# Experts over 512 tokens with a transposed sum, and small work of the attention moved off VectorE

## The chip, the cores and the metric

The kernel runs on one core of a Trainium2 chip. The metric is the time of the core for one execution, in microseconds (us). The engines are PE (TensorE, with PEld for its weight loads), DVE (VectorE), ACT (ScalarE), POOL (GpSimd) and SP (SyncE, which here only issues transfers). Each runs its own list of instructions in order and waits for the others on semaphores.

## The reference

One transformer layer on x of shape (2, 1024, 128): causal attention with 16 heads of 8 dimensions, where the heads of q and k are normalised and rotated, and then a mixture of 16 experts, of which a router picks 2 for each token, beside a shared expert.

```python
x = x + attn(_layernorm(x))
x = x + ffn(_layernorm(x))
# attn: q, k, v = x @ W.T by heads; q, k = layernorm(q), layernorm(k), then rope
scores = where(causal, scale * q @ k.T, -inf); attn = softmax(scores); out = attn @ v @ Wo.T + bo
# ffn: all experts are computed, combine holds the router's two weights of a token
h = silu(xf @ We1 + be1) * (xf @ We3 + be3)
yo = einsum('tei,eid->ted', h, We2) + be2
y = einsum('te,ted->td', combine, yo)
z = silu(xf @ ws1 + bs1) * (xf @ ws3 + bs3) @ ws2 + bs2
```

## The kernel before

The 2048 tokens are four chunks x = 0 to 3 of 512 (two to a sequence). Each chunk passes these stages. Preparation: layernorm, q, k and v, the deviations of the heads (`head_rstd`: an inverse root by three Newton steps on 128 values per partition), rope, and the split of q and k into three bf16 parts that transfers stack up in `q_st` and `k_st`. Attention, in four groups of four heads per chunk, so 16 groups a = 0 to 15: "max" units compute scores with queries on the partitions (L753, L759) and DVE reduces them to row maxima (L1157). DVE negates and splits these (`max_negate`), PE turns them (L770), DVE copies them (`max_copy`, L1176) and a transfer puts them into `q_st` as extra rows, so that the second computation of the scores (L783) comes out with the maximum subtracted. ACT takes the exponential of two banks at once (L911), POOL masks the diagonal, and PE multiplies with v (L801, "pv"). Epilogue: output projection, second layernorm, router (`route1` to `route3`, some 40 small DVE instructions in a chain), and the weights of the experts, which go to memory and come back spread over the partitions (`cstore`, `cload`). Experts: the 16 are 8 pairs, with the shared one 9 units.

Before the change a chunk has 18 expert steps: 9 units for each half of 256 tokens. In each, PE computes the two products U and V into the two halves of one PSUM bank (L838, L839), ACT copies both out with their biases (L948, L950) and takes the tanh (L958), DVE forms (1 + tanh) * U (L1246), V is multiplied with the token's expert weight (L601, on POOL for chunks 0 to 2 and on DVE for chunk 3), POOL multiplies the two (L1076), and PE adds the result into the sum bank with the h tile as stationary operand (L850, two tiles of 128 tokens), so tokens come out on the partitions. The rings of h, U and V hold 4 tiles. The shared expert's two steps come first; the other 16 need the weights from `cload`, which is issued in halves.

The order on each engine is made by a planner in the file, `plan()`: it takes dependences, lengths of each step and an urgency from tables of windows (`PREP_WINDOWS`, `MAX_WINDOWS`, `MOE_WINDOWS`, `PV_LAG`) and writes one list, `SCHEDULE`, from which each engine takes its own steps in order. PSUM has 8 banks: 7 collects pv, 6 the experts' sum, and banks 0 to 5 go to pairs for scores and maxima; single fills (projections, transposes, experts) take 5, 4, 3 or 2. A bank is free again when its reader has read it (`FILLS_READ`).

## Time and profile before

| | |
|---|---|
| three runs | 459.22, 461.11, 461.4 us; median 461.11 |
| the profiled execution | 462.71 us, its span 461.0 us |
| granted TensorE clock, mean | 0.89 of 2.4 GHz |
| busy | PE 387.2, DVE 352.2, ACT 273.4, POOL 186.8 us |
| instructions recorded | 7965 |

The span is the time from the first to the last recorded instruction; 1.7 us of the execution lie outside it. Busy times are of one execution. A matmul's end is modelled in the records, so a PE that shows as full isn't at its peak.

The chain of work that ended last is 55% PE and 25% DVE. The attention's last transposes end near 397 us; what follows is the experts of chunks 2 and 3.

### The profile page before, as it was taken

The numbers are of one execution on the slowest core, as the hardware profiler recorded it, in microseconds if no ns is written. First come the engines' busy times: TensorE is split into PE (matmuls) and PEld (weight loads), VectorE is DVE, ScalarE is ACT, GpSimd is POOL, SyncE is SP. The second block draws the span as 40 slices with busy tenths as digits, with TensorE's granted clock in tenths as the row PEclk, the third lists the DMA queues.
The fourth block names the chain that finished last, engine by engine and source line by source line (L and its number), as shares of the span: only waits on it lengthen the run. The fifth ranks groups of instructions, "written<-read, shape, count | busy, mean of one in ns | idle before, by whom it ended". The sixth has DMA issues, their size and how long they took to land.

```text
span 461.0 us, 7965 instructions
## 1 busy us (share of the span) xinstructions
PE 387.2 (84%) x2663; PEld 194.1 (42%) x2663; DVE 352.2 (76%) x757; ACT 273.4 (59%) x483; POOL 186.8 (41%) x277
## 2 busy tenths in 40 slices
PE   3642867679797999999999798889999999986995
PEld 2321322213323443664334334544333273775884
DVE  4778989889878788794387799987875883678396
ACT  2523044621786584757955664439688789864784
POOL 1303926732065225464523130546202244575564
PEclk9765698575889699999999699999999999999998
DMA  5955022000050007000005005300000000800530
GB/s 144 193 101 137 2 60 79 3 1 0 1 138 1 3 19 169 1 1 1 4 23 139 2 1 126 63 1 1 2 2 0 1 3 4 197 11 1 143 67 23
DMA packets 30265, 21.54 MB, mean 47 GB/s; under 512 B 8945, under 2 KB 30098, under 8 KB 30162
## 3 DMA queue, kind: packets, MB, share of 16 engines
q1 hardware_dynamic: 28834, 19.99, 18.6%
q10 hardware_dynamic: 1392, 1.05, 0.9%
q8 instruction: 22, 0.36, 0.4%
q14 instruction: 17, 0.14, 0.1%
HBM read 13.43 MB, written 1.18 MB: 32 GB/s over the span
## 4 chain that ended last, share of the span: by engine, by line
PE 55%; DVE 25%; ACT 8%; issue 7%; POOL 2%; SPq 1%; DMA 1%; POOLq 0%; ACTq 0%; DVEq 0%
PE psum L801 13%; PE psum L783 7%; PE psum L759 7%; PE psum L850 6%; DVE mx_diag L1157 6%; PE psum L838 6%; PE psum L839 5%; DVE mx_full L1157 3%; PE psum L753 3%; PE psum L724 3%; ACT probs L911 2%; DVE nr L1095 2%; DVE mv L601 2%; DVE nr L1096 2%; PE psum L733 1%
## 5 line engine op out<-in xcount | busy, mean ns | idle before, releaser
L911 ACT ACTIVATE probs<-psum 128x1024 f32<-128x1024 f32 x144 | 141.6, 1027 | 58.7 <-PE psum L783 55.4
L1157 DVE TENSOR_REDUCE mx_diag<-psum 128x4 f32<-128x512 f32 (+2 forms) x96 | 96.6, 1039 | 26.4 <-PE psum L759 25.8
L1065 POOL TENSOR_SCALAR_AFFINE_SELECT probs<-probs 128x256 f32<-128x256 f32 (+1 forms) x112 | 47.7, 442 | 108.3 <-ACT probs L911 107.8
L1157 DVE TENSOR_REDUCE mx_full<-psum 128x2 f32<-128x1024 f32 x64 | 75.8, 1218 | 17.0 <-PE psum L759 16.7
L1076 POOL TENSOR_TENSOR mh<-mh,mv 128x256 f32<-128x256 f32 x72 | 55.5, 777 | 77.9 <-DVE mh L1246 69.5
L801 PE MATMUL psum<-probs,v_ones 128*9 128x512 f32 (+3 forms) x768 | 82.1, 519 | 1.5 <-POOL probs L1065 0.8
L783 PE MATMUL psum<-q_st,k_st 64*128 64x512 bf16 (+3 forms) x384 | 59.8, 363 | 9.7 <-ACT probs L911 6.7
L759 PE MATMUL psum<-k_st,q_st 62*128 62x512 bf16 (+3 forms) x384 | 62.7, 357 | 4.4 <-DVE mx_full L1157 2.3
L1246 DVE SCALAR_TENSOR_TENSOR mh<-mh,mu 128x256 f32<-128x256 f32 x72 | 36.5, 523 | 27.0 <-ACT mh L958 26.7
L948 ACT ACTIVATE mu<-psum,b1h 128x256 f32<-128x256 f32 x72 | 33.8, 470 | 37.0 <-PE psum L839 25.0
L850 PE MATMUL psum<-w,mh 128*128 128x128 f32 x288 | 48.1, 295 | 5.6 <-POOL mh L1076 5.5
L838 PE MATMUL psum<-x2T,w 128*128 128x256 f32 x144 | 47.7, 414 | 1.6 <-ACT mv L950 1.6
L601 POOL TENSOR_TENSOR mv<-mv,comb_b 128x256 f32<-128x256 f32 x48 | 35.4, 740 | 27.7 <-ACT mv L950 23.9
L850 PEld LDWEIGHTS psum<-w,mh 128*128 128x128 f32 x288 | 39.3, 194 | 17.3 <-POOL mh L1076 9.5
L839 PE MATMUL psum<-x2T,w 128*128 128x256 f32 x144 | 43.8, 387 | 0.0
L783 PEld LDWEIGHTS psum<-q_st,k_st 64*128 64x128 bf16 x384 | 17.5, 97 | 59.9 <-ACT probs L911 38.8
L753 PE MATMUL psum<-causal_bf,ident_bf 128*128 128x128 bf16 (+1 forms) x192 | 33.1, 259 | 10.3 <-DVE mx_diag L1157 7.1
L950 ACT ACTIVATE mv<-psum,b 128x256 f32<-128x256 f32 x72 | 33.8, 469 | 0.0
L958 ACT ACTIVATE mh<-mu 128x256 f32<-128x256 f32 x72 | 29.7, 418 | 6.8 <-PE psum L855 2.8
L759 PEld LDWEIGHTS psum<-k_st,q_st 62*128 62x128 bf16 x384 | 16.4, 95 | 35.1 <-issue 16.1
L839 PEld LDWEIGHTS psum<-x2T,w 128*128 128x128 f32 x144 | 28.2, 196 | 4.2
L753 PEld LDWEIGHTS psum<-causal_bf,ident_bf 128*128 128x128 bf16 x192 | 13.4, 101 | 39.1 <-DVE mx_diag L1157 18.6
(142 smaller groups left out, 422.4 us busy)
## 6 DMA issues: line engine op xcount, KB each, us to landing
comb_b<-combine_scratch SPq DMA_DIRECT2D x16, 512.0 KB, 8.7
q_st<-parts SPq DMA_DIRECT2D x24, 128.0 KB, 2.5
k_st<-parts SPq DMA_DIRECT2D x18, 128.0 KB, 2.4
w<-in_We SPq DMA_DIRECT2D x3, 512.0 KB
k_st<-in_c_pad SPq DMA_DIRECT2D x2, 512.0 KB, 8.0
out<-xs SPq DMA_DIRECT2D x4, 256.0 KB, 4.5
xs<-in_x SPq DMA_DIRECT2D x3, 256.0 KB, 10.3
k_st<-parts ACTq DMA_DIRECT2D x6, 128.0 KB, 3.5
```

The source lines that it names most:

```text
L601: engine.tensor_tensor(mv[:, at % MOE_RING, :], mv[:, at % MOE_RING, :], comb_b[:, half, u, :], ALU.mult).then_inc(weighted, 1)
L753: pe.matmul(v, ident_bf[:, :], causal_bf[:, :].unsqueeze(1).broadcast_to([P, nm, P]), start=True, stop=False, skip_group_check=True)
L759: last = pe.matmul(w[:, par, i * keys:(i + 1) * keys], q_st[r, x % 2, 2 * g + m, q0:q0 + P], k_st[r, b, 2 * g + m, k0:k0 + keys], start=(w ...
L783: last = pe.matmul(w[:, par, col:col + cols], k_st[rows(par), b, 2 * g + m, kt * P:(kt + 1) * P], q_st[rows(par), x % 2, 2 * g + m, q0:q0 ...
L801: last = pe.matmul(acc[32 * j:32 * j + VC, q0:q0 + cols], v_ones[:, b, kt, G * g + j, :], probs[:, n % P_RING, j % 2, col:col + cols], sta ...
L838: pe.matmul(w[:, 0:HALF], w1[:, u, :], rhs, start=True, stop=True)
L839: pe.matmul(w[:, HALF:CH], w3[:, u, :], rhs, start=True, stop=True).then_inc(work_full, 1)
L850: last = pe.matmul(y[:, tok * P:(tok + 1) * P], mh[:, at % MOE_RING, t * P:(t + 1) * P], w2[:, u, :], start=(n == 0 and t == 0), stop=(n = ...
L911: act.activation(probs[:, n % P_RING, :, :], wpair("scores", (s, i)), ACT.Exp, scale=SCALE).then_inc(exp_done, 1)
L1065: last = pool.affine_select(out=v, in_=v, compare_op=ALU.is_ge, fill=0.0, base=0, pattern=[[0, v.shape[1]], [1, P]], channel_multiplier=-1)
L1076: pool.tensor_tensor(mh[:, at % MOE_RING, :], mh[:, at % MOE_RING, :], mv[:, at % MOE_RING, :], ALU.mult).then_inc(h_ready, 1)
L1157: dve.tensor_reduce(dst[:, qt, :, pairs[0]:pairs[0] + nm], w, AX.X, ALU.max).then_inc(max_free, 1)
```

## The change

The experts run over all 512 tokens of a chunk at once, 9 units instead of 18 steps. U and V have a bank each (`moeV`, `moeU`). ACT reads V with its bias, halved (`moe_v`); the tanh is read from U's bank, and a second ACT instruction adds 1 (`moe_t`). DVE reads U from PSUM again, adds the bias and multiplies with V (`moe_a`, and this frees U's bank). POOL multiplies with 1 + tanh (`moe_g`), and then POOL, in chunk 3 DVE, multiplies with the expert weight (`moe_h`). The ring of h holds 9 tiles, so a chunk can have all its products ready before its weights arrive. The sum is transposed: the weights w2 are the stationary operand and h the moving one (`moe_sum`), so the sum bank has the output's dimension on the partitions; ACT copies it out (`y_leave`), PE turns it back (`yturn`), DVE adds it. `cload` is two transfers of the whole chunk, not four of halves.

For chunks 1 to 3 the deviations of the heads go from DVE to POOL, in 15 instructions, and rope on POOL is in two steps, so that other steps can stand between. The row maxima are negated by the reduction itself; the split goes to POOL (`max_split`), the copy of the turned maxima to ACT (`mcopy`), and the buffer of the maxima is doubled, so that the next group's reduction waits for the split two groups back. The seed of each inverse root takes one instruction instead of two. All windows of the planner are new.

```diff
-P_RING, MOE_RING = 6, 4
+P_RING, V_RING, T_RING = 6, 4, 9
...
-PV_LAG = 49.3
...
+PV_LAG = 152.8
+WEIGHT_OF = ("moe_h", "moe_h", "moe_h", "moe_h_dve")
+ROPE_OF = (("headrstd", "rope"),) + (("rstd_pool", "rope_pool", "rope_join"),) * 3
...
         def weight(engine, x, n):
 
-            at, (half, u) = 2 * UNITS * x + n, unit(n)
-            if u == 0:
-                engine.wait_ge(ld_combine[half], 32 * (x + 1))
-            engine.wait_ge(act_u, at + 1)
-            engine.tensor_tensor(mv[:, at % MOE_RING, :], mv[:, at % MOE_RING, :], comb_b[:, half, u, :],
-                                 ALU.mult).then_inc(weighted, 1)
+            u = unit(n)
+            if n == 1:
+                engine.wait_ge(ld_combine, 32 * (x + 1))
+            engine.wait_ge(gate_done, UNITS * x + n + 1)
+            h = mh[:, (UNITS * x + n) % T_RING, :]
+            engine.tensor_tensor(h, h, comb_b[:, u, :], ALU.mult).then_inc(weighted, 1)
...
-                rhs = x2T[:, x % 2, half * HALF:(half + 1) * HALF]
-                pe.matmul(w[:, 0:HALF], w1[:, u, :], rhs, start=True, stop=True)
-                pe.matmul(w[:, HALF:CH], w3[:, u, :], rhs, start=True, stop=True).then_inc(work_full, 1)
+                pe.matmul(w, (w1 if kind == "moeU" else w3)[:, unit(n), :], x2T[:, x % 2, :], start=True, stop=True
+                          ).then_inc(work_full, 1)
...
-                pe.wait_ge(h_ready, at + 1)
-                for t in range(2):
-                    tok = 2 * half + t
-                    last = pe.matmul(y[:, tok * P:(tok + 1) * P], mh[:, at % MOE_RING, t * P:(t + 1) * P], w2[:, u, :],
-                                     start=(n == 0 and t == 0), stop=(n == 2 * UNITS - 1), skip_group_check=True)
+                    pe.wait_ge(gate_done, at + 1)
+                else:
+                    pe.wait_ge(weighted, PAIRS * x + n)
+                last = pe.matmul(y, w2[:, unit(n), :], mh[:, at % T_RING, :], start=(n == 0), stop=(n == UNITS - 1),
+                                 skip_group_check=True)
                 if n == BIAS_STEP:
                     pe.wait_ge(work_read_act, frees("act", turned("cT", x)))
-                    for t in range(TPC):
-                        last = pe.matmul(y[:, t * P:(t + 1) * P], combT[:, t * P:(t + 1) * P], b2[:, :],
-                                         start=False, stop=False, skip_group_check=True)
+                    last = pe.matmul(y, b2[:, :], combT[:, :], start=False, stop=False, skip_group_check=True)
                 last.then_inc(y_done, 1)
...
-                if at >= MOE_RING:
-                    act.wait_ge(h_ready, at - MOE_RING + 1)
-                act.activation(mu[:, at % MOE_RING, :], wbank("moe", (x, n))[:, 0:HALF], ACT.Identity,
-                               bias=b1h[:, u:u + 1], scale=0.5)
-                act.activation(mv[:, at % MOE_RING, :], wbank("moe", (x, n))[:, HALF:CH], ACT.Identity,
-                               bias=b3[:, u:u + 1]).then_inc(act_u, 1)
+                if at >= V_RING:
+                    act.wait_ge(gate_done, at - V_RING + 1)
+                act.activation(mv[:, at % V_RING, :], wbank("moeV", (x, n)), ACT.Identity,
+                               bias=b3h[:, unit(n):unit(n) + 1], scale=0.5).then_inc(work_read_act, 1)
...
+                at = UNITS * x + n
+                act.wait_ge(work_full, turned("moeU", (x, n)))
+                if at >= T_RING:
+                    act.wait_ge(y_done, at - T_RING + 1)
+                t = mh[:, at % T_RING, :]
+                act.activation(t, wbank("moeU", (x, n)), ACT.Tanh, bias=b1h[:, unit(n):unit(n) + 1], scale=0.5
+                               ).then_inc(act_t, 1)
+                act.wait_ge(act_t, 2 * at + 1)
+                act.activation(t, t, ACT.Identity, bias=ones_col[:, 0:1]).then_inc(act_t, 1)
...
+                    act.copy(maxT[:, arg % 2, :], wbank("mturn", arg).bitcast(BF16)[0:8, 0:CH]).then_inc(work_read_act, 1)
...
+                elif kind == "y_leave":
+                    act.wait_ge(y_done, UNITS * (arg + 1))
+                    if arg >= 1:
+                        act.wait_ge(work_full, turned("yturn", arg - 1))
+                    act.copy(yT[:, :], bank(Y_BANK)).then_inc(y_left, 1)
...
+            def head_rstd(x):
+                pool.wait_ge(sums_ready, x)
+                y = seed_pool[:, :].bitcast(F32)
+                v, t, h = [nr_pool[:, i, :] for i in range(3)]
+                link(pool.tensor_scalar(v, ssum[:, :], 1.0 / HD, EPS, ALU.mult, ALU.add))
+                link(pool.tensor_scalar(seed_pool[:, :], v.bitcast(I32), -0.5, RSQRT_SEED, ALU.mult, ALU.add))
+                link(pool.tensor_scalar(v, v, -0.5, None, ALU.mult))
+                for step in range(3):
+                    link(pool.tensor_tensor(t, y, y, ALU.mult))
+                    link(pool.tensor_tensor(h, t, v, ALU.mult))
+                    link(pool.tensor_scalar(t, h, 1.5, None, ALU.add))
+                    link(pool.tensor_tensor(y if step < 2 else hrstd[:, :], y, t, ALU.mult))
+
...
+            def max_split(a):
+                c = a // NG % 2
+                if c:
+                    pool.wait_ge(min_ready, NG * (a // NG // 2) + a % NG + 1)
+                else:
+                    pool.wait_ge(max_free, MAXES[a, len(max_units_of(c)) - 1] + 1)
+                m = mx_diag[:, a % 2, :, :, :]
+                if a >= 1:
+                    pool.wait_ge(work_full, turned("mturn", a - 1))
+                hi, lo = [negmax[:, :, :, r, :] for r in range(2)]
+                link(pool.tensor_copy(hi, m))
...
+                    pool.wait_ge(u_read, at + 1)
+                    t = mh[:, at % T_RING, :]
+                    pool.tensor_tensor(t, t, mv[:, at % V_RING, :], ALU.mult).then_inc(gate_done, 1)
...
-                link(dve.tensor_scalar(seed[:, 0:n], v.bitcast(I32), 1, None, ALU.logical_shift_right))
-                link(dve.tensor_scalar(seed[:, 0:n], seed[:, 0:n], -1, RSQRT_SEED, ALU.mult, ALU.add))
+                link(dve.tensor_scalar(seed[:, 0:n], v.bitcast(I32), -0.5, RSQRT_SEED, ALU.mult, ALU.add))
...
+                if u == 0 and a >= 2:
+                    dve.wait_ge(neg_ready, a - 1)
...
-                link(dve.tensor_scalar(hi, m, -1.0, None, ALU.mult))
-                dve.scalar_tensor_tensor(out=lo, in0=m, scalar=-1.0, in1=hi,
-                                         op0=ALU.mult, op1=ALU.subtract).then_inc(neg_ready, 1)
...
+                dve.tensor_reduce(dst[:, a % 2, qt, :, pairs[0]:pairs[0] + nm], w, AX.X, ALU.max, negate=True).then_inc(max_free, 1)
...
+                dve.wait_ge(act_t, 2 * at + 2)
+                v = mv[:, at % V_RING, :]
+                dve.scalar_tensor_tensor(out=v, in0=wbank("moeU", (x, n)), scalar=b1[:, unit(n):unit(n) + 1], in1=v,
+                                         op0=ALU.add, op1=ALU.mult).then_inc(u_read, 1)
...
+                    dve.wait_ge(work_full, turned("yturn", arg))
+                    dve.tensor_tensor(xs[:, arg, :, :], wbank("yturn", arg).rearrange("p (t d) -> p t d", t=TPC),
+                                      xs[:, arg, :, :], ALU.add).then_inc(work_read_dve, 1)
```

The order on DVE before, from the sum of squares of chunk 1 (ssum) to the first groups' maxima (mx_diag); nr, seed and hrstd belong to the deviations of the heads, negmax and maxT to the maxima:

```order
L1128 TENSOR_REDUCE ssum<-sq 128x128
L1132 TENSOR_SCALAR hvar<-ssum 128x128
...
L1097 SCALAR_TENSOR_TENSOR hrstd<-nr,seed 128x128
L1157 TENSOR_REDUCE mx_diag<-psum 128x4 x2
L1157 TENSOR_REDUCE mx_diag<-psum 128x2 x4
L1168 TENSOR_SCALAR negmax<-mx_diag 128x8x2
L1169 SCALAR_TENSOR_TENSOR negmax<-mx_diag,negmax 128x8x2
L1157 TENSOR_REDUCE mx_diag<-psum 128x4 x2
L1176 COPY maxT<-psum 8x512
```

The same place on DVE now:

```order
L1168 TENSOR_REDUCE ssum<-sq 128x128
L1292 MEMSET ones_col 128x1
L1293 TENSOR_SCALAR b3h<-b 128x9
L1294 TENSOR_SCALAR b1h<-b 128x9
L1199 TENSOR_REDUCE mx_diag<-psum 128x4 x2
L1199 TENSOR_REDUCE mx_diag<-psum 128x2 x4
L1199 TENSOR_REDUCE mx_diag<-psum 128x4 x2
L1199 TENSOR_REDUCE mx_diag<-psum 128x2 x4
L1199 TENSOR_REDUCE mx_diag<-psum 128x4 x2
L1199 TENSOR_REDUCE mx_diag<-psum 128x2
L1184 TENSOR_TENSOR resid<-psum,parts 128x512
```

The twelve instructions of the deviations, the two of the split and the copy are gone, and fifteen reductions now stand in a row before the remainder of chunk 1's q (resid).

The order on POOL now at that place, from the last parts of chunk 0 to those of chunk 1 (before, L582 to L593 followed L1047 directly):

```order
L1076 TENSOR_TENSOR parts<-resid,parts 128x512 x2
L1051 TENSOR_SCALAR nr_pool<-ssum 128x128
...
L1058 TENSOR_TENSOR hrstd<-seed_pool,nr_pool 128x128
L587 TENSOR_TENSOR qk<-qk,hrstd 128x1024
L590 TENSOR_TENSOR sq<-qk,g_cos 128x1024
L593 TENSOR_TENSOR roped<-qk,g_sin 128x16x32 x2
L1070 CAST negmax<-mx_diag 128x8x2
L1071 TENSOR_TENSOR negmax<-mx_diag,negmax 128x8x2
L600 TENSOR_TENSOR sq<-sq,g_add 128x1024
L601 TENSOR_TENSOR roped<-roped,sq 128x1024
```

The deviations stand ahead of rope, and the split of group 0's maxima stands between rope's two steps.

The end of PE's order now, from the transpose of chunk 3's expert weights (lg) on; L844 is U or V of a unit, L855 the sum, L859 the biases of the experts, L732 the turn of the sum:

```order
L835 MATMUL psum<-ident,lg 16x128 x4
L855 MATMUL psum<-mh,w 128x512
L844 MATMUL psum<-x2T,w 128x512 x9
L855 MATMUL psum<-mh,w 128x512
L844 MATMUL psum<-x2T,w 128x512 x2
L855 MATMUL psum<-mh,w 128x512
L732 MATMUL psum<-ident,yT 128x128 x4
L855 MATMUL psum<-mh,w 128x512
L859 MATMUL psum<-combT,b 128x512
L855 MATMUL psum<-mh,w 128x512 x7
L732 MATMUL psum<-ident,yT 128x128 x4
```

Before, U and V of chunk 3's steps (L838, L839) alternated with sums (L850) to the end; now all U and V stand ahead of the last eight sums.

## Rows read from the trace of the kernel before

**Rows 1.** Stretches: busy us of PE, PEld, DVE, ACT, POOL; clock, DMA share, GB/s

```profile
40.00:110.00 70.00, 51.48 (x316) 18.10 (x316) 63.33 (x109) 23.46 (x40) 34.70 (x35) 0.70 0.13 32
110.00:160.00 50.00, 44.19 (x304) 17.73 (x302) 39.88 (x90) 31.06 (x49) 20.32 (x25) 0.79 0.12 33
160.00:398.00 238.00, 222.88 (x1706) 104.41 (x1705) 177.66 (x350) 164.78 (x258) 85.41 (x148) 0.97 0.13 32
398.00:461.00 63.00, 52.86 (x304) 45.08 (x302) 44.12 (x110) 40.81 (x104) 38.10 (x50) 0.95 0.26 62
```

**Rows 2.** PE's longest waits, 40 to 110 us and 160 to 250 us: total, times, longest

```profile
PE psum L753 <- DVE mx_diag L1157: 6.5, 10, 2.4
...
PE psum L783 <- ACT probs L911: 1.3, 2, 0.9
```

**Rows 3.** DVE in order of time, 42 to 78 us: start, us, instruction

```profile
42.09 0.23 DVE L1132 TENSOR_SCALAR hvar<-ssum 128x128 f32<-128x128 f32 x1
...
46.43 0.29 DVE L1097 SCALAR_TENSOR_TENSOR hrstd<-nr,seed 128x128 f32<-128x128 f32 x1
...
52.48 0.78 DVE L1168 TENSOR_SCALAR negmax<-mx_diag 128x16 bf16<-128x16 f32 x1
...
55.24 0.40 DVE L1176 COPY maxT<-psum 8x512 bf16<-8x512 bf16 x1
...
76.78 1.29 DVE L1168 TENSOR_SCALAR negmax<-mx_diag 128x16 bf16<-128x16 f32 x1
```

**Rows 4.** POOL in order of time, 21 to 47 us

```profile
21.61 0.45 POOL L566 TENSOR_TENSOR g_add<-g_add,g_tmp 128x128 f32<-128x128 f32 x1
...
46.80 2.34 POOL L582 TENSOR_TENSOR qk<-qk,hrstd 128x1024 f32<-128x1024 f32 x1 [2.85 <-DVE hrstd L1097]
```

**Rows 5.** PE of L838, then L839, then L850 alone, in 160 to 398 us

```profile
160.00:398.00 238.00, 27.27 (x80) 12.85 (x80) 0.97 0.13 32
...
160.00:398.00 238.00, 23.73 (x78) 15.35 (x79) 0.97 0.13 32
...
160.00:398.00 238.00, 26.16 (x152) 20.06 (x152) 0.97 0.13 32
```

**Rows 6.** The chain of waits in order of time: start, us, what; 188 to 189 us

```profile
188.33 0.63 PE psum L838 x2
188.96 0.43 PE psum L839 x2
```

**Rows 7.** The chain of waits, 425 to 461 us

```profile
425.60 0.85 PE psum L827 x4
...
440.00 1.10 PE psum L855 x8
...
443.08 0.86 DVE mv L601
443.95 0.33 DVE mh L1246
...
457.63 0.69 DVE xs L1309
```

**Rows 8.** Issue of chunk 3's expert weights; the page's issues: KB, us to landing

```profile
428.66 4.19 SPq L681 DMA_DIRECT2D comb_b<-combine_scratch  x4
...
comb_b<-combine_scratch SPq DMA_DIRECT2D x16, 512.0 KB, 8.7
```

**Rows 9.** Groups of instructions by shape: busy us, mean ns of one

```profile
L948 ACT ACTIVATE mu<-psum,b1h 128x256 f32<-128x256 f32 x72 | 33.8, 470 | 37.0 <-PE psum L839 25.0 <-POOL mh L1076 11.5
L978 ACT COPY o_raw<-psum 128x512 f32<-128x512 f32 x16 | 9.4, 586 | 15.6 <-PE psum L801 15.5
L1047 POOL TENSOR_TENSOR xs<-xs,bo_b 128x512 f32<-128x512 f32 x4 | 5.1, 1269 | 22.1 <-ACT xn L970 13.3 <-DMA bo_b<-in_bo 8.8
```

**Rows 10.** DVE in order of time, 402 us

```profile
402.04 0.17 DVE L1092 TENSOR_SCALAR seed<-rstd 128x4 int32<-128x4 int32 x1
402.24 0.63 DVE L1093 TENSOR_SCALAR seed<-seed 128x4 int32<-128x4 int32 x1
```

329 lines of the change are left out of this document (155 added, 174 removed).

## The prediction

> **What bounds the kernel now.** I read the stretches first, then the waits of PE, and then the chain. The stretches show three stages with different limits [rows 1]. From 40 to 110 us DVE is busy for 63.3 of 70 us, while the granted clock is 0.70, a mix of the levels 1.2 and 2.4 GHz, and PE's longest wait there is 6.5 us for the maxima that DVE reduces [rows 2]: DVE sets the pace. From 110 to 160 us PE is busy for 44.2 of 50 us at 0.79. From 160 to 398 us it is busy for 222.9 of 238 us at 0.97, and waits little (1.3 us for the exponentials from 160 to 250 us [rows 2]): here only less work on PE helps. In the last 63 us there is no attention any more; PE is busy for 52.9 us, and the chain ends on a rhythm of DVE, 0.86 us for weighting V and 0.33 us for the gate of each step of 256 tokens [rows 7].
>
> **The change part by part.** The terms are against the profiled execution, 461.0 us span and 1.7 us around it.
>
> *Up to 40 us.* The inverse root of chunk 0's heads and the layernorms of chunks 0 to 2 lose one small instruction each on DVE's chain, about 0.2 us (0.17 us and its gap [rows 10]): 4 x 0.2 = -0.8 us. Nothing covers them.
>
> *DVE's stage, 40 to 110 us.* DVE loses the deviations of chunk 1, 42.09 to 46.7 us, so 4.6 us [rows 3], and those of chunk 2, which I take as long: 9.2 us. It loses the splits of four groups; the first row is 0.78 us and its second instruction with gaps 0.25, the third group's 1.29 and 0.25, and for two undisturbed ones I take 0.4 each: 3.4 us. It loses three copies of 0.40 us: 1.2 us. One seed less in chunk 3's layernorm: 0.2 us. Sum 14 us. Two things are late next. POOL needs longer for the deviations: 15 instructions, the nearest row is 0.45 us for 128x128 [rows 4], with gaps 0.5 us each, 7.5 us against 4.6, and chunk 1's rope waits for it. And the split of group 0 stands on POOL behind the three products of rope, 2.34 us the longest of them [rows 4]; PE's turn of these maxima waits for it in PE's order, and the maxima of group 2 are queued behind that turn. POOL would get there at 41.5 + 7.5 + about 6.5 = 55.5 us, PE is there after twelve maxima units from 43.5 us on, near 55 us too. I give back 2 us: -12. The bounds are -14 (all of it on the path) and -4 (each of the two deviations moved hands 5 us back as a wait).
>
> *110 to 160 us.* DVE loses about 6 us more of the same kinds, but PE is busy for 88%: -1, from 0 to -4.
>
> *PE's stage, 160 to 398 us.* L838, L839 and L850 take 27.3 + 23.7 + 26.2 = 77.2 us there [rows 5]. Two recorded pieces make a fp32 matmul, so this is 40 steps of U and V and 38 of the sum, 20 and 19 of the new units. The chain shows the parts of a step: 0.63 us for U, the first product after bf16 work, 0.43 us for V right behind it [rows 6]. 0.43 us is thus 256 columns at the full clock, 0.20 us what the first one after other work pays extra. The sum takes 26.2/38 = 0.69 us per step for 2 x 128 columns, which would be 0.43 us too. A new matmul has 512 columns, 0.86 us, and in this order other work mostly stands ahead of it, so 1.06 us. New: 59 x 1.06 = 62.5 us, so -14.7. The expert biases go from 1.10 us [rows 7] to 0.86: -0.5 for two chunks. Two turns of the sum add about 0.7 us each: +1.4. Sum -13.8 us. What takes some of this back is that U's bank is now held longer: before, ACT read both halves in 2 x 0.47 us [rows 9]; now the bank waits for the tanh, the + 1 (each about 0.47 + 256 x 0.81 ns = 0.68 us, where 0.81 is my slope of the copies of 256 and 512 columns; the copy of 512 takes 0.586 [rows 9]) and DVE's read (0.69 us, as for L1293's kind of 512 from PSUM [rows 7]), 2.05 us and the queues. Of the 13.8 us I take -10. Bounds: -20 and +20.
>
> One rule of the Trainium skill is about the 0.20 us ("TensorE: Matmul & The Clock Gate", section "Step-by-step: what each phase is for"): PE pulls a weight load ahead of a matmul in flight if their rows don't conflict or the load goes to the background buffer. By it the loads of all 59 matmuls could vanish behind the longer ones, 59 x 0.20 = 12 us more. The row shows 0.20 us still open behind bf16 work, and so the sum keeps it.
>
> *The tail.* The last thing that chunk 3 waits for is its expert weights. In the span before, the transpose that leads to them starts at 425.6 us, and the end is 35.4 us later [rows 7]. The four loads are issued from 428.66 us on, over 4.19 us, and land 8.7 us after issue [rows 8], so by about 441 us; two issues for the same bytes land by 440, 14.4 us after that transpose. Before, a step then costs DVE 1.2 us [rows 7], 16 of them 19 us. Now all products of the 9 units wait in the ring of 9, and a unit costs DVE one product of 512, 0.69 us, with POOL idle, and PE 0.86 us: PE sets the pace. From the landing: 0.7 us for the first, 8 x 0.86 and 0.86 for the biases, 7.7; copy out 0.6 [rows 9], turn 0.7, addition 0.7 [rows 7], and the 2.7 us from there to the end that also stand before (457.63 + 0.69 to 461.0); hand-offs 0.6. So 14.4 + 0.7 + 7.7 + 0.6 + 0.7 + 0.7 + 2.7 + 0.6 = 28.1 us, -7.3. Needed for it: ACT has 9 units of 3 x 0.68 = 2.0 us, 18 us, from about 409 us on, plus chunk 2's last; it ends near 435 to 440 us, just in time. POOL has 15 products of chunk 2 and 9 of chunk 3 at 1.27 us, the row for 512 columns [rows 9], 30 us from 397 us on, also in time. I take -7; bounds 0 (ACT is late by 7 us) and -11.
>
> The chain of the layernorm and router of chunk 3, small DVE instructions ahead of that transpose, stays, and here a rule speaks against the change. The rows show one such instruction at 0.17 us and the next, of the same shape, at 0.63 us, at a time when POOL ran its products of 256 columns [rows 10]. The skill ("GPSIMD Engine Reference", section "Specifications") says that POOL shares its SBUF interfaces with VectorE and contends with instructions with two SBUF inputs or in a two-port mode; the trace agrees. It belongs to the rivals, since POOL's products now have 512 columns.
>
> *At no cost or gain*: ACT's three reads per unit (2.0 us per 512 tokens, before 2 x 1.36), the copy of the maxima on ACT (16 x 0.59), the split, hidden while ACT is busy for 165 of 238 us [rows 1]. A copy of maxima that stands behind an exponential on ACT brings its group's scores that much later; PE has other steps in its order there.
>
> Sum: -0.8 - 12 - 1 - 10 - 7 = -30.8 us, 462.7 - 30.8 = 431.9 us. The profiled execution was 1.6 us above the median of the runs shown; against that it is 430 us.
>
> **The rivals.**
> *A, hand-offs give half back, 446 us.* The split and copy of 16 groups go from DVE, right behind the last reduction, to POOL and ACT. For it: PE's order holds the turn at a fixed place, and POOL in order holds rope products of 2.34 us ahead of some. If each turn comes 1 us late and PE waits, 16 us are back. Against it: most groups have a whole group of maxima between split and use.
> *B, U's bank held too long, slower, 470 us.* Mechanism: all of chunks 0 to 2 have their U in one of four single banks, which the pairs for scores and maxima want too; PE in order waits for the bank. Price: 20 units in the long stage, the hold of 2.05 us and DVE's queue of reductions ahead of it, where before it was 0.94. If PE waits 2 us at each, 40 us come back of 30.8: +9, 470 us. It decides from 30.8/20 = 1.5 us a unit on. For it: DVE is busy for 178 of 238 us. Against it: PE waits almost never for a bank today.
> *C, POOL's longer products hold the small DVE chains, 439 us.* A held instruction lasts 0.46 us more than an undisturbed one [rows 10]; behind products twice as wide that is at most twice as much. If five instructions of each of four epilogues are held, an estimate, 5 x 0.46 = 2.3 us is added at each, 9 us if all are on the path.
> *D, weight loads hidden, 418 us.* The 12 us above.
> *E, nothing moves, 461 us.* The new order holds PE's stage at its old length because the planner puts other waits there, and the ends cancel.
>
> **How the numbers follow.** Forecast 430 us (420 to 441 its own range) 0.51; A 0.16; B 0.11; C 0.10; D 0.08; E 0.04. I let the range reach from 415 us, below D, to 454 us, beyond A; B, E and the far side of A are outside. Faster by over 0.5% (that much, 2.3 us, is what a measurement can tell from no change): 0.51 + 0.16 + 0.10 + 0.08 = 0.85. Within 0.5%: 0.04. Slower: 0.11.
>
> **What would show it.** Right: the first reductions 2 us or more earlier (they now start behind the row at 46.43 us [rows 3]), and 12 us gained by the end of DVE's stage; U, V and sums of PE together 62.5 us for as many units as take 77.2 now; a tail with eight sums in a row, 28 us from the transpose of the expert weights to the end. Wrong: waits of PE for the split on POOL or for U's reader on DVE of over 10 us in total, a PE below 90% from 150 us on, or ACT as the engine that the last sums wait for.

## The result, and the profile after

The changed kernel takes 456.32 us (median of 4, 455.38 to 457.29) against 461.25 us of the kernel before on the same chip: ratio 0.9887, 95% interval 0.9853 to 0.9921. It is faster by 1.1%, some 5 us, where 30 us were forecast.

First the stretches of the changed kernel, in the columns of [rows 1]. The bounds are set by marks: at 390.0 us the last transpose of the attention's raw output (o_raw) is done, at 425.4 us PE turns chunk 3's router table.

```profile
40.00:110.00 70.00, 56.98 (x366) 21.16 (x366) 53.59 (x81) 29.81 (x54) 52.20 (x79) 0.74 0.13 32
110.00:160.00 50.00, 42.36 (x334) 14.24 (x336) 35.54 (x86) 38.30 (x51) 28.50 (x46) 0.93 0.12 33
160.00:390.00 230.00, 213.62 (x1431) 72.11 (x1424) 158.53 (x273) 154.94 (x201) 80.56 (x128) 0.98 0.13 29
390.00:425.40 35.40, 29.86 (x79) 12.98 (x78) 23.58 (x69) 20.84 (x35) 17.75 (x16) 0.89 0.30 60
425.40:455.00 29.60, 23.56 (x56) 9.51 (x54) 11.93 (x18) 12.44 (x20) 11.35 (x9) 0.96 0.43 90
```

And of the kernel before, between the same marks, which there lie at 396.1 and 426 us:

```profile
160.00:396.10 236.10, 221.20 (x1694) 102.94 (x1693) 176.35 (x346) 163.43 (x255) 85.41 (x148) 0.97 0.13 31
396.10:426.00 29.90, 24.33 (x139) 19.98 (x139) 22.91 (x75) 18.28 (x47) 18.11 (x24) 0.97 0.24 55
426.00:461.00 35.00, 30.21 (x179) 26.57 (x176) 22.52 (x39) 23.87 (x62) 19.99 (x27) 0.94 0.32 77
```

Three things stand in these rows. The attention ends 6.1 us earlier, which is all that was won. From its end to the turn of the table the changed kernel takes 5.5 us more (35.4 against 29.9), and from there to the end 5.4 us less: the two cancel, 64.9 us both times. And PE is busy for 382.1 us in all, 5.1 us less than before, though its weight loads fell by 55 us, from 194.1 to 138.7.

The early part gained as much as was forecast. The first 30 of the 160 reductions of maxima are done at 91.8 us instead of 103.6. But of these 11.8 us only 6.1 are left when the attention ends. Most of the loss has one place: the 70th reduction is still 10.4 us earlier than before (179.2 for 189.6 us), the 80th only 2.7 (204.5 for 207.2), the last 7.6. From the 70th reduction to the end of the attention, which is PE's stage, the kernel before takes 206.5 us and the changed one 210.8.

### The profile page after: what moved, and what is told of

It is laid out like the page before. It is cut to its first block, busy times and chain, and to the rows that moved or that the text cites. A ratio compares the mean times of both kernels' runs of the same rounds, so it can differ in the third digit from the quotient of the medians.

```text
span 454.9 us, 6876 instructions
## 1 busy us (share of the span) xinstructions
PE 382.1 (84%) x2295; PEld 138.7 (30%) x2295; DVE 309.4 (68%) x622; ACT 269.6 (59%) x395; POOL 198.7 (44%) x294
## 4 chain that ended last, share of the span: by engine, by line
PE 48%; DVE 16%; ACT 10%; DMA 8%; issue 7%; POOL 7%; SPq 2%; ACTq 1%; POOLq 0%; DVEq 0%
PE psum L809 11%; PE psum L791 7%; PE psum L844 6%; PE psum L855 6%; PE psum L767 6%; DMA comb_b<-combine_scratch 5%; DVE mx_full L1199 5%; ACT probs L917 4%; PE psum L732 3%; PE psum L761 3%; DVE mx_diag L1199 3%; PE psum L741 1%; ACT sq L934 1%; PE psum L859 1%; DMA xs<-in_x 1%
## 5 line engine op out<-in xcount | busy, mean ns | idle before, releaser
L1111 POOL TENSOR_SCALAR_AFFINE_SELECT probs<-probs 128x256 f32<-128x256 f32 (+1 forms) x112 | 47.6, 442 | 90.4 <-ACT probs L917 87.9
L844 PE MATMUL psum<-x2T,w 128*128 128x512 f32 x144 | 77.1, 639 | 5.8 <-ACT mv L954 2.7
L1121 POOL TENSOR_TENSOR mh<-mh,mv 128x512 f32<-128x512 f32 x36 | 45.6, 1270 | 76.6 <-DVE mv L1271 76.6
L855 PE MATMUL psum<-mh,w 128*128 128x512 f32 x72 | 42.6, 693 | 6.0 <-POOL mh L610 3.4
L1271 DVE SCALAR_TENSOR_TENSOR mv<-psum,b,mv 128x512 f32<-128x512 f32 x36 | 26.4, 745 | 23.6 <-ACT mh L966 23.5
L963 ACT ACTIVATE mh<-psum,b1h 128x512 f32<-128x512 f32 x36 | 24.7, 686 | 23.1 <-PE psum L844 23.1
L954 ACT ACTIVATE mv<-psum,b3h 128x512 f32<-128x512 f32 x36 | 24.5, 682 | 21.1 <-PE psum L844 21.0
L844 PEld LDWEIGHTS psum<-x2T,w 128*128 128x128 f32 x144 | 24.2, 196 | 32.6 <-issue 14.0
L610 POOL TENSOR_TENSOR mh<-mh,comb_b 128x512 f32<-128x512 f32 x24 | 30.3, 1269 | 8.2 <-DMA comb_b<-combine_scratch 6.9
L933 ACT COPY qk<-psum 128x256 f32<-128x256 f32 x16 | 6.0, 378 | 36.6 <-POOL roped L601 20.1
L966 ACT ACTIVATE mh<-mh,ones_col 128x512 f32<-128x512 f32 x36 | 26.0, 722 | 1.2
L809 PEld LDWEIGHTS psum<-probs,v_ones 128*9 128x9 f32 x768 | 13.7, 89 | 35.3 <-issue 32.1
## 6 DMA issues: line engine op xcount, KB each, us to landing
xs<-in_x SPq DMA_DIRECT2D x3, 256.0 KB, 10.2
```

Of the source, the lines that this page charges most:

```text
L610: engine.tensor_tensor(h, h, comb_b[:, u, :], ALU.mult).then_inc(weighted, 1)
L809: last = pe.matmul(acc[32 * j:32 * j + VC, q0:q0 + cols], v_ones[:, b, kt, G * g + j, :], probs[:, n % P_RING, j % 2, col:col + cols], sta ...
L844: pe.matmul(w, (w1 if kind == "moeU" else w3)[:, unit(n), :], x2T[:, x % 2, :], start=True, stop=True).then_inc(work_full, 1)
L855: last = pe.matmul(y, w2[:, unit(n), :], mh[:, at % T_RING, :], start=(n == 0), stop=(n == UNITS - 1), skip_group_check=True)
L1111: last = pool.affine_select(out=v, in_=v, compare_op=ALU.is_ge, fill=0.0, base=0, pattern=[[0, v.shape[1]], [1, P]], channel_multiplier=-1)
L1121: pool.tensor_tensor(t, t, mv[:, at % V_RING, :], ALU.mult).then_inc(gate_done, 1)
```

## Why fewer and wider matmuls gave nothing

The forecast took 14.7 us off U, V and the sum. I counted them again from the records of all matmuls, each from its start to the start of the next one (or to its own end, if PE then waits), so that no time is counted twice:

| us of PE, whole kernel | before | after |
|---|---|---|
| U and V | 71.3 | 72.2 |
| the sum | 41.6 | 40.0 |
| biases of the experts, turn of the sum | 4.3 | 7.7 |
| together | 117.2 | 119.9 |

The groups that the forecast read add up to far more: U and V 91.5 us and the sum 48.1 in the kernel before. The reason is in the timeline. Here is PE of the kernel before (start, us, instruction):

```profile
191.03 0.70 PE L838 MATMUL psum<-x2T,w 128*128 128x256 f32 x2
191.56 0.59 PE L839 MATMUL psum<-x2T,w 128*128 128x256 f32 x2
192.09 0.39 PE L783 MATMUL psum<-q_st,k_st 64*128 64x512 bf16 x2
192.41 0.71 PE L850 MATMUL psum<-w,mh 128*128 128x128 f32 x4
193.05 0.39 PE L759 MATMUL psum<-k_st,q_st 62*128 62x512 bf16 x2
```

U is shown with 0.70 us, but V starts 0.53 us after it: the records overlap, since the end that is modelled for a matmul lies after the start of the next one. U and V together hold PE from 191.03 to 192.09, 1.06 us, not 1.29. PE of the changed kernel:

```profile
284.42 1.13 PE L844 MATMUL psum<-x2T,w 128*128 128x512 f32 x2
285.48 0.39 PE L767 MATMUL psum<-k_st,q_st 62*128 62x512 bf16 x2
285.80 1.12 PE L855 MATMUL psum<-mh,w 128*128 128x512 f32 x2
286.85 0.39 PE L778 MATMUL psum<-ident_bf,negmax 128*8 128x128 bf16 x4
```

A matmul of 512 columns holds PE for 1.06 us, as long as U and V of 256 did together. I call a row of fp32 matmuls between bf16 ones a visit. Each of these matmuls is recorded as two pieces. Inside a row of them a piece of 512 columns starts 0.429 us after the one before, so 512 columns cost 2 x 0.429 = 0.857 us. At the full clock, with no wait beside them, the visits of both kernels have these medians:

| columns in the visit | before | after | left over at 0.857 us per 512 columns |
|---|---|---|---|
| 256 (sum of one step) | 0.644 (22 of them) | | 0.22 |
| 512 | 1.063 (11) | 1.058 (24) | 0.21, 0.20 |
| 1024 | 1.927 (4) | 1.916 (3) | 0.21, 0.20 |

So a visit costs its columns and 0.2 us once, whatever the number of matmuls. The 0.2 us has two halves: the first piece behind a bf16 matmul takes 0.533 us to the next start, the last piece ahead of a bf16 matmul 0.525, all between them 0.429. For 512 tokens U and V were two visits of 512 columns before (one for each half) and are two after: nothing can be won. The sum, where it stands by itself, went from two visits of 0.64 to one of 1.06 us, 0.23 us less; for all 36 units that would be 8 us. Its time fell by 1.6 us only: 9.3 us of it now lie at the low clock, 1.9 before, which is 3.7 us, and before, in the tail, many sums already stood in one long visit. In the whole kernel, work of the experts stands right behind a bf16 matmul 55 times before and 49 times after, so only six openings went away. Biases and turns take 3.4 us more. The Trainium skill ("TensorE: Matmul & The Clock Gate", section "Step-by-step: what each phase is for") has PE pull a weight load ahead of a running matmul; within a visit the trace agrees, since the loads that went away cost nothing, and only the 0.1 us at its head and the 0.1 us at its end stay open.

PE's whole work can be put in one number: busy time less half of what fell into stretches granted 1.2 GHz. The halving is an estimate, from a sum that takes 2.07 us at the low clock and 1.13 at the full one (shown further down). Before it is 387.2 - 75.9/2 = 349.2 us, after 382.1 - 63.2/2 = 350.5. PE waits 70.4 us before and 69.3 after (end of the last matmul less its busy time). The gain thus lies almost all in the clock.

## The experiments

All ran with the kernel before beside them on the same chip. Ratios are to it, with 95% intervals.

| run | us, median | ratio |
|---|---|---|
| changed kernel again | 457.86 | 0.9892 (0.9854 to 0.993) |
| loads in halves | 446.95 | 0.9663 (0.9623 to 0.9703) |
| POOL's products in pieces of 256 | 461.4 | 0.9987 (0.9942 to 1.0031) |
| relief of DVE taken back | 468.53 | 1.0122 (1.0075 to 1.0169) |
| only the splits taken back | 464.0 | 1.0066 (1.0027 to 1.0104) |
| kernel before, relief only | 480.43 | 1.0422 (1.0365 to 1.0479) |
| chunk 3's gate products small | 455.21 | 0.9853 (0.9814 to 0.9892) |
| loads in quarters | 447.19 | 0.9681 (0.9629 to 0.9732) |
| halves, U right behind V | 472.85 | 1.0225 (1.0167 to 1.0283) |
| chunk 3's weights loaded early | 455.71 | 0.9877 (0.9839 to 0.9916) |
| halves, chunk 2's products small | 437.94 | 0.9492 (0.9449 to 0.9535) |
| halves, chunk 2's weights on DVE | 440.81 | 0.9559 (0.9512 to 0.9605) |

### The changed kernel again

> The changed kernel itself, once more, as the mark for the three beside it: 0.989 of before, 456 us, with the same places in its trace: PE's work as before, chunk 3's expert weights 12 us in landing.

It came out as expected and is the mark for the others. Its chain of chunk 3's router is 14.1 us long where the first trace has 15.6, and its tail 1.5 us longer: PE waits 2.78 us for chunk 3's first weighted product, not 1.81, and is then granted 1.2 GHz for 3.4 us. Two traces of one kernel can thus differ by 1.5 us in one stage, and smaller differences between single traces say little.

### The loads in halves

```diff
-                    for e in range(2):
-                        src = combine_dram[x].rearrange("(m e) q -> e m q", e=2)[e]
-                        sp.dma_start(comb_b[64 * e:64 * e + 64, :, :], src.partition_broadcast(64)
-                                     ).then_inc(ld_combine, 16)
+                    for part in range(2):
+                        for e in range(2):
+                            p = slice(part * PAIRS // 2, (part + 1) * PAIRS // 2)
+                            src = combine_dram[x].rearrange("(m e) q -> e m q", e=2)[e, p]
+                            sp.dma_start(comb_b[64 * e:64 * e + 64, p, :], src.partition_broadcast(64)
+                                         ).then_inc(ld_combine[part], 16)
...
-            if n == 1:
-                engine.wait_ge(ld_combine, 32 * (x + 1))
+            if n in (1, 1 + PAIRS // 2):
+                engine.wait_ge(ld_combine[n > 1], 32 * (x + 1))
```

> The changed kernel with each load of expert weights cut in two by pairs (first pairs 0 to 3, then 4 to 7), in the same order of all other work. Theory 1 (the end is a chain of waits with the load of 12 us in it twice: chunk 2's load holds PE's sum, and the gate of chunk 3 stands behind that sum in PE's order; then chunk 3's load): the first half lands after some 8 us, the gate of chunk 3 comes 3 to 4 us earlier, and of the last load 1 to 3 us are saved, since the second half lands as late as now but only four sums are left: 4 to 6 us under the changed kernel, about 451 us. Theory 2 (the load is hidden, the units of ACT and POOL are what the last sums wait for): within 1 us of the changed kernel.

This edit moves nothing else, and takes 10.6 us off (0.9892 - 0.9663 of 461.8), twice what was expected. The chain behind it starts at chunk 0. POOL of the changed kernel waits for the load. It is one piece of two issues, which has nothing to use until both have landed, 13.0 us after the first issue; with halves the first part can be used after 9.0 us:

```profile
173.44 1.27 POOL L1121 TENSOR_TENSOR mh<-mh,mv 128x512 f32<-128x512 f32 x1 [3.10 <-DVE mv L1271]
178.14 2.48 POOL L610 TENSOR_TENSOR mh<-mh,comb_b 128x512 f32<-128x512 f32 x2 [3.43 <-DMA comb_b<-combine_scratch]
```

PE of the changed kernel, in the same stretch:

```profile
177.56 0.39 PE L767 MATMUL psum<-k_st,q_st 62*128 62x512 bf16 x2
179.45 2.07 PE L855 MATMUL psum<-mh,w 128*128 128x512 f32 x2 [1.50 <-POOL mh L610]
181.46 2.07 PE L859 MATMUL psum<-combT,b 17*128 17x512 f32 x2
183.46 1.04 PE L767 MATMUL psum<-k_st,q_st 62*128 62x512 bf16 x4
```

and with the loads in halves:

```profile
176.45 0.39 PE L769 MATMUL psum<-k_st,q_st 62*128 62x512 bf16 x2
176.77 1.13 PE L857 MATMUL psum<-mh,w 128*128 128x512 f32 x2
177.83 1.12 PE L861 MATMUL psum<-combT,b 17*128 17x512 f32 x2
178.88 0.61 PE L769 MATMUL psum<-k_st,q_st 62*128 62x512 bf16 x4
```

PE waits 1.50 us, and the clock that it is granted falls to 1.2 GHz at 178.9 us for 10.2 us, in which a sum takes 2.07 instead of 1.13 us. With halves there is no such wait and no fall. The stretch of 160 to 200 us as a whole, first of the changed kernel, where the granted clock is 0.87:

```profile
160.00:200.00 40.00, 37.17 (x164) 12.21 (x160) 29.38 (x34) 18.56 (x26) 14.59 (x14) 0.87 0.27 54
```

and with halves, where it is 1.00 and PE gets 202 matmuls done instead of 164:

```profile
160.00:200.00 40.00, 38.46 (x202) 12.62 (x199) 32.69 (x37) 23.24 (x31) 15.03 (x16) 1.00 0.27 54
```

The wait of 1.5 us with the clock behind it thus costs about 6 us here: with halves the 70th reduction of maxima is done 1.1 us earlier than in the changed kernel, the 80th 6.8 us earlier. How much such a wait costs isn't fixed. With the relief of DVE taken back (below) PE waits 1.59 us at the same sum and is then granted 1.2 GHz for 3.4 us only; with the splits alone taken back it waits 1.77 us, and it is 6.8 us. From the 70th reduction to the end of the attention the kernel with halves takes 206.3 us, against 210.8 in the changed kernel and 206.5 before. The rest was expected. In the changed kernel PE's order has the gate of chunk 3 behind a sum of chunk 2, and this sum waits for chunk 2's load:

```profile
405.20 1.13 PE L855 MATMUL psum<-mh,w 128*128 128x512 f32 x2 [1.89 <-POOL mh L610]
406.25 1.12 PE L859 MATMUL psum<-combT,b 17*128 17x512 f32 x2
407.31 1.67 PE L827 MATMUL psum<-w_o,x2T 128*128 128x16 f32 x8
```

The chain of waits of the changed kernel has the two loads with their full length (start, us, what):

```profile
391.72 12.09 DMA comb_b<-combine_scratch
...
428.67 12.29 DMA comb_b<-combine_scratch
```

With halves the time from the end of the attention to the turn of the router table is 3.3 us shorter than in the trace of the changed kernel again, and from there to the end another 3.2 us, of which 1.5 are that trace's longer tail. The page's line of issues, of the changed kernel

```profile
comb_b<-combine_scratch SPq DMA_DIRECT2D x8, 1024.0 KB, 10.0
```

stands against [rows 8]: two issues bring as many bytes as four did, but nothing may start before all are there.

### The loads in quarters

> The changed kernel with each load of expert weights in four parts of two pairs each. Theory 1 (what counts is when the first pairs are there; the queue moves 2 MB in 10 us however it is cut): the first part lands after 4 to 6 us, the waits of sums for chunks 0 and 2 stay away as with halves, and the last load gives 0 to 2 us more, because its last part lands as late as now and only two sums are left: 445 to 447 us. Theory 2 (more and smaller transfers cost their own time on the queue): 448 to 451 us.

447.19 against 446.95 us: theory 1. A part lands after 5.9 us (median from its issue). Once the first pairs are in time, smaller pieces add nothing.

### The relief of DVE taken back, whole and in part

In the changed kernel `max_split`, and in the first run the inverse roots too, go back to DVE, where the order has them:

```diff
+            def max_split(a):   # on DVE
+                ...
+                link(dve.tensor_copy(hi, m))
+                dve.tensor_tensor(lo, m, hi, ALU.subtract).then_inc(neg_ready, 1)
...
+                elif kind == "rstd_pool":
+                    head_rstd(arg)   # on DVE; POOL's rope waits for it
```

> The changed kernel with the inverse roots of chunks 1 to 3 and all splits of maxima back on DVE, at the same places of the order; the transposed sum, the copy of the maxima on ACT, the negated reductions and the shorter seed stay. Theory 1 (all of the gain comes from the relief of DVE up to 110 us, by less idle time of PE and fewer stretches at the low clock; the transposed experts give nothing): the lead of 5 to 6 us that the changed kernel has there goes, 461 to 463 us. Theory 2 (the gain is the tail's, the relief is off the path): 456 to 458 us.

> The changed kernel with only the splits of the maxima back on DVE; the inverse roots stay on POOL. Taking both back cost 10.6 us. Theory 1 (what counts is the DVE time taken off up to 110 us, 9.2 us of roots and 3.4 us of splits): the splits are worth 2 to 4 us, 459 to 461 us. Theory 2 (on POOL the split waits as long as it took on DVE): within 1 us of the changed kernel, 456 to 458 us.

Both back cost 10.6 us (1.0122 - 0.9892), more than the expected 5 to 6; the splits alone cost 8.0 us (1.0066 - 0.9892), against 2 to 4 expected, so both theories on them fall short. The first 30 reductions are done at 95.8 us instead of 91.9 with both back, but at 90.4 with the splits alone, whose loss comes late: 3.9 us at the last reduction, 6.1 us at the end of the attention. PE waits 9 and 6 us more up to 390 us. With the splits alone, PE's waits for a split on DVE rise to 8.4 us in all, where for POOL's they were 1.7: on DVE the split stands behind reductions of other groups. This speaks for the place of the splits in the order, more than for the DVE time taken off, but which of the late waits cost what was not taken apart. The roots by themselves would be worth the difference, 2.6 us, but the two intervals overlap, so that this is not shown.

### The kernel before with the relief alone

The same moves of roots and splits to POOL, put into the kernel before at the places of its own order.

> The kernel before, its experts untouched, with only the relief of DVE: inverse roots of chunks 1 to 3 and all splits of maxima on POOL, the reductions negated, the shorter seed; the copy of turned maxima stays on DVE, the order of all stages is that of before. Theory 1 (the relief alone is worth about what taking it away cost the changed kernel, 10 us, and the transposed experts by themselves give nothing): 451 to 455 us. Theory 2 (PE's order of before holds the splits at places that fit DVE and not POOL, the relief shows only with an order made for it): 459 to 465 us.

It is 19.5 us slower than before: theory 1 fell, and theory 2 was too mild. PE's longest waits in it:

```profile
PE psum L773 <- POOL negmax L1060: 16.7, 2, 9.5
PE psum L804 <- POOL probs L1098: 12.1, 5, 5.7
```

Two turns of maxima wait 16.7 us for a split on POOL. POOL in order of time shows why:

```profile
58.53 2.34 POOL L596 TENSOR_TENSOR roped<-roped,sq 128x1024 f32<-128x1024 f32 x1
60.81 0.20 POOL L1059 CAST negmax<-mx_diag 128x16 bf16<-128x16 f32 x1
61.09 0.22 POOL L1060 TENSOR_TENSOR negmax<-mx_diag,negmax 128x16 bf16<-128x16 f32 x1
```

The 0.4 us of the split stand behind 20 us of roots, bias and rope, for which PE waits 9.5 us; a second split, behind rope of chunk 2, is done at 98.9 us in the same way, and PE has waited 7.2 us for it. This is the mechanism of the forecast's rival A. In the changed kernel it doesn't happen, since the new windows put the splits ahead of rope's second half: its PE waits 1.7 us for them.

### What holds chunk 3's router

The router's chain of 38 small DVE instructions takes 11.5 us for chunk 3 before and 15.6 us after. DVE of the changed kernel:

```profile
410.29 1.17 DVE L1244 TENSOR_TENSOR lg<-lg,red 128x64 f32<-128x64 f32 x1
411.50 1.19 DVE L1245 TENSOR_TENSOR lg<-lg,gate_bb 128x64 f32<-128x64 f32 x1
412.72 1.29 DVE L1249 TENSOR_TENSOR pair_sums<-lg 128x48 f32<-128x48 f32 x1
...
417.81 0.17 DVE L1219 TENSOR_REDUCE red<-gsm 128x4 f32<-128x16 f32 x1
```

and its POOL at the time:

```profile
410.12 1.26 POOL L610 TENSOR_TENSOR mh<-mh,comb_b 128x512 f32<-128x512 f32 x1
411.34 1.27 POOL L1121 TENSOR_TENSOR mh<-mh,mv 128x512 f32<-128x512 f32 x1
412.69 1.26 POOL L610 TENSOR_TENSOR mh<-mh,comb_b 128x512 f32<-128x512 f32 x1
```

> The changed kernel with every product of an expert unit on POOL as two instructions of 256 columns, in the same order. Theory 1 (a small DVE instruction is held until POOL's running product ends, up to 1.1 us for 512 columns): the router chain of chunk 3, 15.6 us from its first reduction to its last product in the changed kernel and 11.5 us before, goes back to 12 to 13 us and its held instructions last 0.6 us at most instead of 1.2; the end is 2 to 4 us earlier, 453 us. POOL is busy 17 us more. Theory 2 (these instructions are long for a reason of their own): chain and length stay at 15.6 and 1.2 us, and the time stays or rises by up to 2 us.

> The changed kernel with the nine gate products of chunk 3 on POOL cut from 512 to 16 columns (the rest of chunk 3's hidden values is left out, so the output is not the reference's), the order the same. Theory 1 (POOL's running products hold the small DVE instructions of chunk 3's router): the router chain goes from 14.1 to 15.6 us to 10 to 11 us as in chunks 0 and 1, at most two instructions over 0.4 us, and the end comes 3 to 4 us earlier, 453 us. Theory 2 (the hold is of another making): chain over 13 us and time within 1 us of the changed kernel.

Neither edit shortened the chain. In pieces of 256 columns (two `tensor_tensor` for one) the held instructions last 0.79 us at most instead of 1.3, but there are 12 of them instead of 6: the chain is 14.06 us against 14.14 in the changed kernel again. The whole is 4.4 us slower, more than theory 2 allowed; POOL is busy for 8.9 us more, but what of this lies on the path was not taken apart. In both kernels every held instruction ends 0.03 to 0.08 us after the end of a POOL product, as theory 1 has it: DVE's 411.50 + 1.19 = 412.69 above stands against POOL's 411.34 + 1.27 = 412.61. Its mechanism holds, its gain doesn't come, because a hold of half the length is met twice as often. What helps is less of POOL's work beside the chain. And with chunk 3's gate products cut to 16 columns the chain stays at 15.6 us (theory 2; the time, 1.8 us lower by the ratios, has intervals that overlap): chunk 3's products run later. What runs beside the router is chunk 2's, L610 and L1121 in turn from 403.9 to 419.1 us, queued up behind chunk 2's load. So the next two runs took those:

```diff
+            c = slice(0, 16 if x == 2 else CH)   # products small, both kinds
...
-                elif kind == "moe_h_dve":
+                elif kind == "moe_h_dve" or (kind == "moe_h" and arg[0] == 2):   # weights on DVE
                     weight(dve, *arg)
```

> The kernel with halved loads, all products on POOL of chunk 2's units cut to 16 columns (chunk 2's hidden values are left out in part). Theory 1 (it is these products, queued up behind chunk 2's load, that run beside chunk 3's router and hold its small DVE instructions; chunk 3's own run later): the router chain of chunk 3 goes from 15.1 to 9 to 10.5 us, with no instruction over 0.65 us, and the time falls by 3 to 5 us against the halved loads alone, to 442 to 444 us. Theory 2 (something else makes them long): 14 us or more, and the time stays at 447.

> The kernel with halved loads, chunk 2's expert weights multiplied in on DVE instead of POOL, at the same places of the order. Theory 1 (POOL's products beside the router are halved in number, and DVE, idle for half of that stretch, takes 0.69 us for one): the router chain of chunk 3 goes from 15.1 to 11 to 13 us, the time to 443 to 446 us. Theory 2 (the products on DVE stand in front of the router in its order and wait for the load there): 447 to 452 us.

With small products the chain is 9.06 us and no instruction in it lasts over 0.26; the time falls by 7.9 us against the halves alone (0.9663 - 0.9492), more than the 3 to 5 expected. The chain gives 6.0 us of it. PE's wait for the router table is also gone (4.70 us with halves), and with it a stretch of 6.8 us at 1.2 GHz that starts at 413.3 us with halves. With chunk 2's weights on DVE the chain is 10.9 us, three weights of 0.65 us included, a little shorter than the 11 to 13 us expected. DVE of that kernel, the same instructions:

```profile
401.33 0.25 DVE L1247 TENSOR_TENSOR lg<-lg,red 128x64 f32<-128x64 f32 x1
401.61 0.23 DVE L1248 TENSOR_TENSOR lg<-lg,gate_bb 128x64 f32<-128x64 f32 x1
401.87 0.21 DVE L1252 TENSOR_TENSOR pair_sums<-lg 128x48 f32<-128x48 f32 x1
```

0.25 us instead of 1.17. This kernel leaves nothing out, and at 440.81 us (0.9559), below the expected 443 to 446, it beats both kernels, by 4.4% and by 3.4%.

### U right behind V

```diff
-            add("moeU", (x, n), key, ("moeV", (x, n)))
+            add("moeU", (x, n), -1e6, ("moeV", (x, n)))
```

> The halved loads, and U's matmul forced right behind V's of the same unit in the order (the order of much else shifts with it). Theory 1 (a visit of fp32 work between bf16 work pays 0.2 us, and the change only made two visits of one column block out of two visits of two): PE's time for U and V, counted from the start of one matmul to the start of the next, falls from 72 to 66 to 68 us, and PE's whole work by the same amount; the end is up to 5 us earlier than with the halves alone, if the new order doesn't wait more. Theory 2 (the 0.2 us belongs to each weight load, wherever it stands): U and V stay at 71 to 73 us.

On the time it missed: 472.85 us. The order of nearly everything shifts, the attention ends 34 us later than with halves alone, and PE waits 13 us more. On PE's work it leans to theory 1: U and V hold PE for 76.1 us, of which 16.5 at the low clock, 67.8 if these are halved, against 70.7 - 1.9/2 = 69.8 in the kernel with quarters, whose U and V stand mostly apart. Its expert work stands behind a bf16 matmul 37 times, with halves 49 times; 12 openings of 0.2 us are 2.4 us. The visits of 1536 columns in it have 2.774 us, 3 x 0.857 and 0.20. The medians of visits above show the law better than this run does. While its chunk 3's router runs, POOL has nothing to do, and the chain takes 9.06 us, as with small products.

### Chunk 3's weights loaded early

Chunk 3's load takes chunk 2's table, as soon as chunk 2's weights are used up.

> The changed kernel, chunk 3's expert weights loaded from chunk 2's table as soon as chunk 2's are used up, so that the last load doesn't wait for chunk 3's router (chunk 3 is weighted wrongly). Theory 1 (the last sums wait for this load, which lands 441 us into the span): its units are ready 2 to 5 us before that on ACT and POOL, the end comes 3 to 5 us earlier, 452 to 454 us. Theory 2 (the units come late all the same, ACT's last pass over them ends at 440 us): within 1 us of the changed kernel.

The end moves by 0.0015 of 461, under 1 us: theory 2. In its trace PE doesn't wait for the first weighted product, for which it waits 1.81 us in the changed kernel, and the last seven sums start at 442.0 us instead of 443.8. More isn't won, as PE's order has all of chunk 3's U and V and chunk 2's last turn ahead of these sums. In the tail the load is hidden but for these 1.8 us.

## Why the prediction was wrong

*What bounds the kernel*: nothing speaks against the three stages, and DVE's stage did gain.

*Up to 40 us, -0.8*: the turn of chunk 0's heads ends 0.3 us earlier (33.9 for 34.2 us). Small and not separated further.

*DVE's stage, -12, and 110 to 160 us, -1*: the size is about right, with some luck in its working. The early maxima are 11.8 us earlier. But roots and splits were to give 12.6 of the 14 us there, and with both back on DVE the first 30 reductions come only 3.9 us later; with the splits alone back they come 1.5 us earlier. The other 7.9 us must lie in the copy on ACT, the doubled buffer and the new order, which no run takes apart. Roots and splits do matter by the end, 10.6 us, but most of that arises later. The other bound, that what moves comes back as a wait, is what the kernel before shows with these moves alone (+19.5 us); the new order avoided it. As the forecast had it, PE is at the turn of group 0's maxima near 55 us, and its wait there is 1.5 us.

*PE's stage, -10*: this is the step that failed. "L838, L839 and L850 take 27.3 + 23.7 + 26.2 = 77.2 us there" summed busy times that overlap each other. The chain beside them gave 0.63 + 0.43 = 1.06 us for U and V of a step [rows 6], while [rows 5] over 40 steps make 1.28; the two rows disagreed and I used the larger for the old kernel and the smaller for the new. 40 x 1.06 + 38 x 0.64 = 66.7 us would have stood against the 62.5 of the new: -4.2 instead of -14.7, and -3.3 with the forecast's own terms for biases and turns, before anything is given back. Counted from start to start, the groups of [rows 5] hold PE for only 40.7 + 22.8 = 63.5 us in that stretch, a gain of 1 us. What the stage did as a whole agrees: between the 70th reduction and the end of the attention the kernel with halves, which has no long wait for the load, takes 206.3 us and the kernel before 206.5, where the forecast took 10 us off, and this although in this stretch the kernel before is granted 1.2 GHz for 13.6 us and the one with halves for 3.4. The 0.20 us per visit was read rightly in size, but put down to U alone (U and V start 0.53 us apart, and the next matmul 0.53 us after V); and the new units open as many visits for U and V as before.

*U's bank held* (rival B, and the give-back of 4 us): of no weight. PE waits 1.1 us in all for its reader on DVE.

*The tail, -7*: the stretch forecast at 28.1 us took 29.9, so -5.4. The load landed at 441 us, 1 us after the forecast, and the last seven sums ran in a row at 0.86 us. PE of the changed kernel:

```profile
443.84 6.28 PE L855 MATMUL psum<-mh,w 128*128 128x512 f32 x14
450.79 0.66 PE L732 MATMUL psum<-ident,yT 128*128 128x128 f32 x4 [0.68 <-ACT yT L1035]
```

But the same amount was lost just ahead of it, at the gate and in the router. Rival C named that mechanism and priced it at up to 9 us over four epilogues; in fact the router's chains of chunks 0 and 1 got shorter (10.0 us for 11.8 and 11.1), chunk 2's is the same within 0.3 us, and chunk 3 alone lost 4.1 us (2.6 in the second trace).

*Not in the forecast at all*: that of a load in one piece nothing can be used until 13 us after its first issue, where the kernel before had its first half after 8 to 10 us. The forecast's 8.7 us is the median from issue to landing of single issues; each last issue landed 12 us after its issue in chunks 0 to 2 before as well. I followed the load in the tail, where it is nearly hidden, and not to chunks 0 and 2, where PE's order has sums close behind it. It costs 10.6 us.

*The rivals*: A's mechanism is real (+19.5 us in the kernel before) but stayed at 1.7 us here, B's and D's did not show. Rival E, with a chance of 0.04, came nearest: the new order put another wait into PE's stage, the one for the load, and the two ends cancel.

Put together: the relief is worth -10.6 us and the load in one piece costs +10.6, each measured against the changed kernel; what is left for all the rest is the measured -5, which is a remainder and not a measurement of its own. Of this rest the wider units' part was not run by itself: no kernel here has them in the order of before.

## What to carry to other kernels

Take a matmul's price from start to start of its neighbours, or from the chain, never from a sum of group busy times, and check that the prices of one step agree between two views. Fewer, wider instructions win only the fixed part that is still open between them; count these openings before and after. When transfers are merged, follow the first consumer of each one through the order of every engine: the edits of a few lines there (loads in halves, chunk 2's weights on DVE) took off another 3.4%, three times what the whole change won.

## What the runs showed of the hardware

- A PE that waited 1.5 us between busy stretches was granted half the clock for 10.2 us, and some 6 us were lost; in the same place without the wait the clock stayed at 1.00. Waits of 1.59 and 1.77 us at this place in two other runs were followed by 3.4 and 6.8 us at half the clock.
- fp32 matmuls in a row start 0.429 us apart for each piece of 512 columns at the full clock, although each piece has a weight load of its own. The change from bf16 to fp32 and the one back cost 0.10 us each.
- Small DVE products of two SBUF operands (0.17 to 0.25 us alone) last up to 1.3 us while POOL works on products of 512 columns, up to 0.79 us beside products of 256, with the same length of the chain (14.14 and 14.06 us); a reduction between them keeps its 0.17 us. Each held one ends within 0.08 us after POOL's running product. The Trainium skill ("GPSIMD Engine Reference", section "Specifications") says that POOL contends with VectorE's instructions that have two SBUF inputs. The traces agree, and show in addition that cutting POOL's instructions in two gives nothing back.
- A load of 2 MB from memory spread over the partitions kept the queue busy for 11.0 us in one piece and 11.1 in halves (chunk 0), some 190 GB/s; only the moment of the first usable part changed.
